# Attention scores in float32r on the two halves of the TensorE array, in place of stacked bf16 rows

## The reference

```python
qkv = _gn(x).reshape(bs, 1024, 192) @ w_qkv          # 12 heads of 16
attn = softmax(einsum('bhqd,bhkd->bhqk', q, k) * 16 ** -0.5)
x = x + (einsum('bhqk,bhkd->bhqd', attn, v) ... ) @ w_o
x = x + layer2(_gn(x))     # rfft2, two complex block matmuls with relu, irfft2, plus a linear part
```

## Time and profile before

| | |
|---|---|
| runs | 1689.0, 1689.3, 1699.71 us; median 1689.3 |
| profiled execution, first to last instruction | 1693.3 us |
| PE busy | 1619.6 us (96%) |
| DVE busy | 1242.5 us (73%) |
| ACT busy | 980.5 us (58%) |
| POOL busy | 235.2 us (14%) |
| mean granted PE clock | 0.977 |

### The profile page before, as it was taken

How to read it: one execution, slowest core, us unless ns; L and a number is a source line. 1 busy time by engine, 2 the same in 40 slices (tenths; PEclk the granted TensorE clock), 3 DMA queues, 4 the chain that set the end, 5 groups by cost and what they waited for, 6 DMA issues and landing times.

```text
span 1693.3 us, 28191 instructions
## 1 busy us (share of the span) xinstructions
PE 1619.6 (96%) x8580; PEld 692.3 (41%) x8580; DVE 1242.5 (73%) x2236; ACT 980.5 (58%) x1837; POOL 235.2 (14%) x297
## 2 busy tenths in 40 slices
PE   8999999999999999999999999999999999999877
PEld 4233334344343444344343443434444444434345
DVE  2887888777778767877678777877788777787132
ACT  4275776665656655666556665666566666666401
POOL 3001001410104001130013100141011300030010
PEclk9699999999999999999999999999999999999989
DMA  4501113134313134041240430422430412310323
GB/s 109 82 20 38 16 39 82 27 58 83 81 22 58 35 78 101 3 73 48 49 101 2 83 73 14 101 32 54 83 78 7 74 47 48 82 27 22 66 42 77
DMA packets 110733, 93.81 MB, mean 55 GB/s; under 512 B 27632, under 2 KB 96624, under 8 KB 110576
## 3 DMA queue, kind: packets, MB, share of 16 engines
q1 hardware_dynamic: 110576, 91.86, 27.2%
HBM read 14.32 MB, written 6.29 MB: 12 GB/s over the span
## 4 chain that ended last, share of the span: by engine, by line
PE 67%; issue 14%; DVE 6%; POOL 4%; SPq 3%; DMA 3%; ACT 1%; POOLq 0%; DVEq 0%; ACTq 0%
PE o_acc L1168 17%; PE scores L1134 16%; PE max_tiles L1148 15%; DVE row_max L902 3%; PE prep_bank L1239 3%; PE prep_bank L1191 2%; PE post_bank L1303 2%; PE post_bank L1297 2%; SPq L584 2%; PE post_bank L1203 2%; PE post_bank L1310 2%; DMA rows_b<-rows_a 1%; PE post_bank L1289 1%; PE post_bank L1210 1%; PE post_bank L1191 1%
## 5 line engine op out<-in xcount | busy, mean ns | idle before, releaser
L902 DVE TENSOR_REDUCE row_max<-max_tiles 128x1 f32<-128x512 f32 x1536 | 972.6, 680 | 208.7 <-PE max_tiles L1148 205.5
L805 ACT ACTIVATE probs<-scores 128x512 f32<-128x512 f32 x1536 | 837.2, 596 | 368.6 <-PE scores L1134 362.9
L1134 PE MATMUL scores<-q_stack,k_stack 98*128 98x512 bf16 x1536 | 587.3, 384 | 3.1 <-ACT probs L805 2.6
L1148 PE MATMUL max_tiles<-k_stack,q_stack 96*128 96x512 bf16 x1536 | 581.8, 388 | 6.0 <-DVE row_max L902 4.3
L1168 PE MATMUL o_acc<-probs,v_aug 128*32 128x512 f32 x3072 | 413.1, 610 | 13.1 <-ACT o_raw L813 11.9
L1134 PEld LDWEIGHTS scores<-q_stack,k_stack 98*128 98x128 bf16 x1536 | 150.3, 98 | 381.7 <-ACT probs L805 254.7
L1148 PEld LDWEIGHTS max_tiles<-k_stack,q_stack 96*128 96x128 bf16 x1536 | 152.7, 99 | 181.3 <-DVE row_max L902 76.0
L463 POOL TENSOR_TENSOR o_raw<-o_raw,inv_all 128x1024 f32<-128x1024 f32 x23 | 54.2, 2356 | 763.8 <-DVE inv_all L930 763.8
L1168 PEld LDWEIGHTS o_acc<-probs,v_aug 128*32 128x32 f32 x3072 | 60.8, 108 | 160.0 <-issue 144.2
L735 POOL TENSOR_TENSOR qk_parts<-rest,qk_parts 128x512 bf16<-128x512 f32 x48 | 55.5, 1156 | 404.3 <-DVE qk_parts L960 404.3
L1239 PE MATMUL prep_bank<-xt,w_qk 96*128 96x512 f32 x172 | 80.8, 592 | 0.0
(11 more groups left out here) (220 smaller groups left out, 1114.4 us busy)
## 6 DMA issues: line engine op xcount, KB each, us to landing
q_stack<-qk_parts SPq DMA_DIRECT2D x288, 64.0 KB, 2.6
k_stack<-qk_parts SPq DMA_DIRECT2D x144, 128.0 KB, 4.5
rows_b<-rows_a SPq DMA_DIRECT2D x128, 96.0 KB, 3.2
spec_b<-spec_a SPq DMA_DIRECT2D x64, 102.0 KB, 2.3
x_in<-in_x_dram SPq DMA_DIRECT2D x8, 768.0 KB, 5.8
o_t<-o_raw SPq DMA_DIRECT2D x96, 64.0 KB, 2.4
x<-in_x_dram SPq DMA_DIRECT2D x8, 768.0 KB, 6.8
rows_b<-spec_b SPq DMA_DIRECT2D x32, 192.0 KB, 3.3
```

The source lines that it names most:

```text
L805: nc.scalar.activation(probs[:, GH * (s % 2) + h, :], scores[:, n % SCORE_BANKS, :], ACT.Exp, scale=SCALE).then_inc(probs_made, 1)
L902: nc.vector.tensor_reduce(row_max[:, which, pair_of_half:pair_of_half + 1], max_tiles[:, no % MAX_BANKS, :], AX.X, ALU.max).then_inc(max_t ...
L1134: mm(scores[:, n % SCORE_BANKS, :], k_stack[:, head, P * kt:P * (kt + 1)], q_stack[:, g, half, h, :], start=True, stop=True).then_inc(scor ...
L1148: mm(max_tiles[:, no % MAX_BANKS, :], q_stack[0:KQ, g, half, h, P * qt:P * (qt + 1)], k_stack[0:KQ, GH * g + h, HALF * which:HALF * (which ...
```

## The change

- q and k are split in two parts of dtype float32r (four bytes), not three of bf16. `Q_PARTS = (0, 0, 1)`, `K_PARTS = (0, 1, 0)`: 48 rows a head in place of 96. Part 1 is written straight by the subtraction on DVE; the cast on DVE and the subtraction on POOL are gone, and so are their semaphores.
- Even heads of the stacks lie on partitions 0 to 49, odd heads on 64 to 113. The columns of the q/k weights are permuted so that each half can be copied by one DMA. The stack DMAs stay 6 for each call: 3 products x 2 halves. The shifts take 4 DMAs, not 2.
- The score matmul reads 50 rows (`rows`), the maximum matmul 48, on the half of its head. The order of maximum tiles is changed by `max_unit` so that each comes on the half which the neighbouring score matmul doesn't use: in issue order a step is max odd, score even, max even, score odd, `pv`, job 1, score even, max odd, score odd, max even.
- The ones under the k parts are a DVE memset of all `k_stack`, in place of twelve ACT instructions.

```diff
-Q_PARTS = (0, 0, 0, 1, 1, 2)
-K_PARTS = (0, 1, 2, 0, 1, 0)
+Q_PARTS = (0, 0, 1)
+K_PARTS = (0, 1, 0)
...
-        qk_parts = sb("qk_parts", [P, 3, 3, TOK], BF16)
-        rest = sb("rest", [P, 2, HALF])
-        q_stack = sb("q_stack", [KQ + 2, NG, 2, GH, HALF], BF16)
-        k_stack = sb("k_stack", [KQ + 2, NH, TOK], BF16)
+        qk_parts = sb("qk_parts", [P, 2, 3, TOK], F32R)
+        q_stack = sb("q_stack", [P, NG, 2, GH // 2, HALF], F32R)
+        k_stack = sb("k_stack", [P, NH // 2, TOK], F32R)
...
+        def max_unit(unit, i):
+
+            half, m = divmod(unit, HUNITS)
+            hp, qt = divmod(m, NT // 2)
+            return half, hp, qt, 1 - i % 2, i // 2
...
-                for n in range(2):
-                    sp.dma_start(q_stack[KQ + n:KQ + n + 1, g, half, :, :],
-                                 shift[:, n, :]).then_inc(shift_in, 16)
+                for n, odd in itertools.product(range(2), range(2)):
+                    row = 64 * odd + KQ + n
+                    sp.dma_start(q_stack[row:row + 1, g, half, :, :].bitcast(F32),
+                                 shift[HMAX // 2 * odd:HMAX // 2 * (odd + 1), n, :].bitcast(F32)
+                                 ).then_inc(shift_in, 16)
...
-            def last_part(b, k):
-
-                pool.wait_ge(part1_done, 6 * b + k + 1)
-                cols = slice(HALF * (k % 2), HALF * (k % 2 + 1))
-                nc.gpsimd.tensor_tensor(qk_parts[:, 2, k // 2, cols], rest[:, k % 2, :],
-                                        qk_parts[:, 1, k // 2, cols], ALU.subtract
-                                        ).then_inc(part2_done, 1)
...
-                if kind == "second_part":
-                    prep_taken(dve, b, "qk", k)
-                    cols = slice(HALF * (k % 2), HALF * (k % 2 + 1))
-                    nc.vector.tensor_copy(qk_parts[:, 1, k // 2, cols], rest[:, k % 2, :]
-                                          ).then_inc(part1_done, 1)
...
-                    nc.vector.tensor_tensor(rest[:, k % 2, :], bank_,
-                                            qk_parts[:, 0, k // 2, cols],
+                    nc.vector.tensor_tensor(qk_parts[:, 1, k // 2, cols], bank_,
+                                            qk_parts[:, 0, k // 2, cols].bitcast(F32),
                                             ALU.subtract).then_inc(prep_by_dve, 1)
...
+                nc.vector.memset(k_stack[:, :, :].bitcast(F32), 1.0).then_inc(stack_ones, 1)
...
-                head = GH * g + h
-                mm(scores[:, n % SCORE_BANKS, :], k_stack[:, head, P * kt:P * (kt + 1)],
-                   q_stack[:, g, half, h, :],
+                hp, odd = divmod(h, 2)
+                rows = slice(64 * odd, 64 * odd + KQ + 2)
+                mm(scores[:, n % SCORE_BANKS, :], k_stack[rows, 2 * g + hp, P * kt:P * (kt + 1)],
+                   q_stack[rows, g, half, hp, :],
                    start=True, stop=True).then_inc(scores_made, 1)
...
-                mm(max_tiles[:, no % MAX_BANKS, :], q_stack[0:KQ, g, half, h, P * qt:P * (qt + 1)],
-                   k_stack[0:KQ, GH * g + h, HALF * which:HALF * (which + 1)],
+                rows = slice(64 * odd, 64 * odd + KQ)
+                mm(max_tiles[:, (TILES * g + no) % MAX_BANKS, :],
+                   q_stack[rows, g, half, hp, P * qt:P * (qt + 1)],
+                   k_stack[rows, 2 * g + hp, HALF * which:HALF * (which + 1)],
                    start=True, stop=True).then_inc(max_made, 1)
```

More of the change, by code:

```diff
@@ L29 @@
 from contextlib import ExitStack
+import itertools
 import concourse.bass as bass
@@ L38 @@
 F32 = mybir.dt.float32
-BF16 = mybir.dt.bfloat16
+F32R = mybir.dt.float32r
 P = 128
@@ L856, in prologue @@
             def prologue():
-                act.wait_ge(cleared, 3)
-                for head in range(NH):
-                    nc.scalar.activation(k_stack[KQ:KQ + 2, head, :], inv_all[KQ:KQ + 2, :],
-                                         ACT.Identity, bias=1.0).then_inc(stack_ones, 1)
                 for no, (kind, k) in enumerate(PREP):
@@ L913, in split_shift @@
                 dve.wait_ge(shift_turned, halves(b, g, half) + 1)
-                after(dve, shift_in, 32 * halves(b, g, half))
-                turned = prep_bank[0:HPAIRS, 0, 0:P]
+                after(dve, shift_in, 64 * halves(b, g, half))
+                turned = prep_bank[0:HMAX, 0, 0:P]
                 nc.vector.tensor_scalar(shift[:, 0, :], turned, -1.0, None,
@@ L1057, in prologue @@
                     place_v(0, g)
-                for n in range(2 * AHEAD):
-                    if n == HPAIRS:
+                for unit in range(AHEAD):
+                    if unit == HUNITS:
                         split_shift(0, 0, 0)
-                    for which in range(2):
-                        take_max(n // PAIRS, n // PAIRS, n % PAIRS, which)
+                    for i in range(4):
+                        take_max(0, 0, unit, i)
             def body(b, prep, post):
@@ L1069, in body @@
                     jobs = jobs_of(b, u, prep, post, prep_piece, post_piece)
[L1070 removed]
+                    tiles = unit_ahead(b, u, prep)
                     if jobs:
                         jobs[0][0](*jobs[0][1:])
[L1073 to L1076 removed]
+                    for tile in tiles[:2]:
+                        take_max(tile[0], *tile[2:])
                     for job in jobs[1:]:
                         job[0](*job[1:])
[L1079 to L1082 removed]
+                    for tile in tiles[2:]:
+                        take_max(tile[0], *tile[2:])
                     if u in shift_steps(prep):
@@ L1382, in prologue @@
                 keep_busy(BUSY[4])
-                pe.wait_ge(stack_ones, NH)
                 pe.wait_ge(cleared, 6)
-                for n in range(2 * AHEAD):
-                    slot, pair = divmod(n, PAIRS)
-                    for which in range(2):
-                        max_tile(slot, 0, slot, pair, which)
-                    if n == HPAIRS - 1:
+                for unit in range(AHEAD):
+                    for i in range(4):
+                        max_tile(0, 0, 0, unit, i)
+                    if unit == HUNITS - 1:
                         turn_shift(0, 0, 0, (0, *PREP[-1]))
@@ L1396, in body @@
                     jobs = jobs_of(b, u, prep, post, prep_piece, post_piece)
-                    pairs = pairs_ahead(b, u, prep)
-                    tiles = [(*pair, which) for pair in pairs for which in range(2)]
+                    tiles = unit_ahead(b, u, prep)
                     if jobs:
```

95 lines of the change are left out of this document (40 added, 55 removed).

## The result

The changed kernel takes 1710.8 us in the median (1694.7 to 1728.1, 14 runs), the kernel before beside it 1691.5 (1683.6 to 1704.2, 14 runs). The ratio is 1.0083, 95% interval 1.0051 to 1.0116: a little slower, within the 1% that I called no change, where 1615 had been forecast. Two of the changed kernel's 14 runs (1728.1 and 1721.6 us) are in a slower state and don't enter the ratio. The profiled execution has a span of 1706.4 us, 13.1 more than before, and a mean granted clock of 0.946 (0.977 before).

A forecast was written before the change was run, and what follows sets the result against it. PE bounds steps with a job, ACT and two score banks bare steps. 14.0 - 1.5 (DVE) - 2.0 (SP) = 10.5 us a body, times 7 is 74, so 1619 profiled and 1615 median (chance 0.60); range 1570 to 1740.

The forecast's parts named there:

- a pair costs 0.22: Score and maximum matmuls: two float32r matmuls on both halves at once take 0.22 us, not 0.44; four pairs replace eight matmuls.
- for work side by side: Pairs on two row halves: nearest row is `pv`, whose four column strips load and stream together; bounds 0.22 and 0.44.
- pairs take turns: Rival for the score and maximum matmuls: halves don't overlap, a pair costs 0.44, time 1824 us; chance 0.20.
- stream like float32: Rival for the score and maximum matmuls: 0.86 us a matmul even in pairs, about 2600 us; chance 0.05.
- Changes of array mode: PE switching between half arrays, `pv` strips and whole-array jobs: 0.09 us a change, new on both sides of job 0.
- the job's exposed load 0.08: Job 0 behind pairs: 0.08 us where its 128-column float32 weight load can't hide.
- A float32r load lies between ... I take 0.04: Weight load, between bf16 99 ns and float32 189: 0 to 0.08 us longer where exposed, 0.04 taken.
- 14.0 - 1.5 = 12.5: Gain a body: 14.0 us summed over steps with and without jobs, less an estimated 1.5 for DVE.
- No faster PE shortens this ring: Steps without a job: bound by ACT's exponentials and two score banks at 2.93 us, so gain only in steps with a job.
- 2 x 0.04 = 3.01: Steps without a job: the ring of 2.93 us plus two exposed float32r loads of 0.04.
- SP: 1.2 + 0.8 = 2.0 a body: Two more shift DMAs on SP: 1.2 us at step 29 before mixing, 0.8 in group 0; range 0 to 3.
- (A) to (C): Experiments' theories: float32r load exposed in every pair group; remaining gain ends in SP-set waits; lower clock behind costs more.

## Why the prediction was wrong

It said 10.5 us a body; bodies 2 to 6 gained 0.5, and body 7 lost 24.4. Of the 10 us that are missing in a body, 7.7 are missing in the steps where the pairs should have gained and 2.3 in those that SP rules; body 7 is the clock. By its own steps:

**"a pair costs 0.22", "for work side by side":** right. The partners start within 0.01 us, in bf16 pairs are 0.22 to 0.23 apart, and float32r streams in 0.235. The rivals in which pairs take turns, or stream like float32, are out. From the 3.07 times for four row tiles that the Trainium skill has ("TensorE: Matmul & The Clock Gate", Part 3) I had estimated 0.28 a pair at worst; the bf16 rows are at 0.23.

**"Changes of array mode", "the job's exposed load 0.08":** right in size. The job costs 1.91 for 1.71: 0.20, and the sum had 0.08 + 0.09 + 0.04 = 0.21.

**"A float32r load lies between ... I take 0.04":** this is the step that failed first, a mis-sized term. The load is not between the two rows, it is the float32 one (190 ns). Each group of two pairs costs 0.67 (895.14 to 895.81 before the job, 897.72 to 898.39 after it), where the sum has 0.53 + 0.04 = 0.57 before the job and 0.53 after it, its 0.04 being in the job's 0.21. So a q/k step gains 0.31, not 0.54. Outside the steps that SP rules, 4.8 us a body were gained where 14.0 - 1.5 = 12.5 were forecast; of the 7.7 that are missing, bf16 in the same kernel gives back 6.4 in the 41 steady steps, and loses 1.4 of it in step 45. I had the bytes as an argument for float32 and the single pass for bf16; for the load the runs decide for the bytes. The Trainium skill ("TensorE: Matmul & The Clock Gate", Weight-path perf modes) gives the fast load to 128 weights of a dtype that is not FP32; by that the float32r load would be fast, and the rows, 190 ns against 94 in bf16, disagree.

**"No faster PE shortens this ring", "2 x 0.04 = 3.01":** the sentence holds within 0.05 us, the size doesn't. Cut as in the prediction, from `pv` to `pv`, the bare steps 4 and 7 of bodies 2 to 6 take 2.93 before and 3.09 to 3.10 after: 0.16 more, twice the 0.08 of an exposed float32 load, where the sum has twice 0.04. With bf16 halves, and a PE that is faster in the steps with a job, they take 2.88 to 3.01.

**DVE and POOL:** DVE's busy time fell by 2.4 us, not by 17 ("near 1225"). The casts took 20.0 us away; one memset of `k_stack` puts 5.2 back, the copies into `v_aug` 4.4 (619 ns each for 438), and the 48 combinations of maxima (`full_max`) 3.1 (250 ns for 185). Why the same copies take longer wasn't tried, and the remaining 4.9 weren't placed. What POOL's 55 us were worth wasn't tried apart; the sum has nothing for them. DVE is late next, as the 0.24 wait in the bf16 kernel shows. How much of the rest of the 7.7 is DVE's wasn't separated.

**"SP: 1.2 + 0.8 = 2.0 a body":** step 31 is right: 1.10 more, and 1.23 back with two shift DMAs. In group 0 the 0.8 is right as the price of the shifts (0.75 back) and wrong as the whole: steps 8 to 10 lose 3.15. The rest is a missing term. `o_raw` comes free by a chain of DMAs on SP that doesn't get shorter when PE does: `pv` of step 9 starts 34.3 us behind the first exponential of its body before and 34.2 after, in the mean of bodies 2 to 6. So what PE saves in steps 0 to 8, 0.5 us, is waited for in step 9, and the greater part, some 2.6, is lost behind the wait to the lower clock. I had the wait's row in hand, and used it only to price the shifts; that row is of body 4, and bodies 2 and 3 had waits of 3.10 and 3.66 already.

**Not in the forecast at all: the clock.** Behind the wait of 3.07 us in body 4 the clock is 0.51 for 12.7 us. The length of the wait alone doesn't decide it: behind 3.49 us in body 6 steps 8 to 10 have 0.90, behind 2.27 in body 5 0.67. With the gap filled by useless work the kernel is 1.8% faster (1.0083 to 0.9903). Body 7 with its 0.86 is 24.4 us longer, more than the span's 13.1. The Trainium skill ("TensorE: Matmul & The Clock Gate", Part 1) says that an idle TensorE falls to the lower clock; behind the waits the rows agree. The sum has no term for the clock; it takes the 0.977 of before as it is.

**What stays open.** Body 7 took 165.6 to 179.8 us in nine kernels of the table and 199.4 and 188.7 in the two with four shift DMAs and float32r; why the clock is low there for 54.6 us in all, behind waits of 0.7 to 2.9 us, was not separated. That body decides whether the kernel is slower than before or level with it, so the loss of 0.8% is explained in part only; the gain that is missing elsewhere is explained by (A) to (C). And why the lower clock lasts longer with matmuls on half the rows: one half alone has 0.77, the whole array in the same dtype 0.982, with the same matmuls on other rows, in one run each.

## What to carry to other kernels

Where short groups of matmuls stand between other work, price their first weight load by its own row. Here it went with the number of bytes of the dtype, not with the number of passes. When an engine gets faster, look for the waits that already end at something it can't speed up (here a DMA chain in the order of one queue) and subtract the saved time there; what stands ahead in that queue and could stand behind can be worth more than the change, as here (2.8% against 1.6%). Read such a wait in every body, not in one. A wait of TensorE costs more than its length if the granted clock falls behind it, so read the clock in the windows behind each long wait before and after.

## What the hardware did that I had not expected

- A float32r load of 128 columns takes 190 ns whether it has 48 or 114 rows, a bf16 one 94 ns on 50 rows and 98 on 98.
- The first two float32r matmuls of a group are 0.34 apart and the next ones 0.235, on one half or the whole array.
- Two matmuls on the upper and lower rows, writing two banks, start within 0.01 us, and the next two follow 0.22 to 0.23 later in bf16.
- The granted clock stayed at 0.50 for 88.7 us in which TensorE worked without a pause, on one half of the rows; over that run it was 0.77.
- Six useless matmul records in a wait of 0.7 to 3.5 us, in each of six bodies, made a kernel 1.8% faster, partly by a body in which none stood.
- A wait of 2.27 us was followed by a granted clock of 0.67 over three steps, one of 3.49 by 0.90, in the same kernel.
